# The joint of a ternary feed-forward stage and a windowed attention stage: closing order, values, a sum of squares and a table load moved

## The chip, the cores and the metric

The kernel runs on one core of a Trainium2 chip. The metric is the device time of one execution in microseconds (us). Five engines share the work: TensorE (PE, matmuls), VectorE (DVE), ScalarE (ACT), GpSimd (POOL) and SyncE (SP, which only issues DMAs here).

## What is computed

The input X is 4096 rows of 256 (two sequences of 2048). Four residual parts follow one another: a retention network of two layers with its feed-forward parts, a ternary feed-forward part, a windowed attention, and the same ternary feed-forward part again. Cut to what the change touches:

```python
def _ternary_linear(x, w):
    ...
    rms = jnp.sqrt(jnp.sum(x * x, axis=-1, keepdims=True)) / jnp.sqrt(jnp.asarray(d, x.dtype))
    x_norm = x / (rms + EPS)
    return jnp.einsum('bsd,fd->bsf', x_norm, w_q)
h = jax.nn.gelu(_ternary_linear(x, w_up), approximate=False)
return _ternary_linear(h, w_down)
...
q = _rms_norm(q)
k = _rms_norm(k)
q = _apply_rotary(q, cos, sin)
k = _apply_rotary(k, cos, sin)
...
att = jax.nn.softmax(scores, axis=-1)
y = jnp.einsum('bhqk,bhkd->bhqd', att, v_full)
...
x = x + _L0_ffn_ref(_layernorm(x, axis=-1), L0_ffn_w_up, L0_ffn_w_down)
x = x + _L0_attn_b_ref(_layernorm(x, axis=-1), ...)
x = x + _L0_ffn_ref(_layernorm(x, axis=-1), L0_ffn_w_up, L0_ffn_w_down)
```

The attention has 16 query heads and 4 key heads of 16 columns and looks back 64 rows.

## The kernel before

X stays in on-chip memory. Every stage is a block of one program for each engine, and the stages follow one another: a stage begins when every engine has finished the one before (the joint). Inside a stage the order on each engine is written out by hand, and semaphores couple the engines. POOL collects the engines at a joint and lets them go.

**The ternary stage** (`ffn`, called with `window` for the first of the two) walks over NB = 8 blocks of 512 rows. A step g works on block b = g - 2 on the hidden side and normalises block g - 1; each step has MF = 8 parts m, one for 128 of the 1024 hidden columns. For a part, PE makes the hidden product (L857), ACT applies Gelu twice (L758, L759), DVE subtracts (L548), and PE adds the part to the output (L870, `down_product`) two parts later. Beside that ACT and POOL square the hidden values; PE adds the squares over the rows with ones (L905, `square_sums`, in two halves), ACT copies the result (L787), PE transposes it (L919, `transpose_sums`), DVE copies it (L560), POOL takes its root (L448, L452), and DVE takes the reciprocal (L566) and adds the scaled output into X (L577, four instructions of 256 columns).

**At its end** this stage already does work of the attention, which takes tiles of 128 rows; tiles 0 and 1 are begun here. For each of them PE projects queries, keys and values (L929, `first_project`), and ACT takes the squares (L793) and a raw copy (L796, `first_raw`). For tile 0 DVE sums the squares (L641), POOL takes the power -0.5 of 20 columns (L356) and multiplies by a gain (L359, `first_head_scales`), DVE rotates (L650, L653, L662) and writes the scaled heads (L666, `first_pad`). POOL copies the values of both tiles in three instructions each (L366, L369, L372, `first_values`).

In step 10 (`NB + 2`), the last but one, the written order on PE is: part 6 of the last block's output product, second half of the square sums, part 7 of the output product, transpose of the sums, projection of tile 1. DVE's order is: output of block 6 (L577), rotation (at m = 3), copy of the sums (L560, m = 5), `first_pad` (m = 6), then in step 11 reciprocal and output of block 7. The function `closing(g)` is true only in the last stage, and gives there another order by `last_down`.

**The attention stage** (`window_attention`, NT = 32 tiles) runs step n with tiles in different phases: `project` (L2589) of tile n - 2, keys and queries transposed by PE (L2608, L2619) and copied by ACT (L2460, L2454) for tile n - 3, keys moved by POOL (`even_keys`, L2230, L2231) for tile n - 3, `head_scales` by POOL (L2218, L2222) for n - 2, `pad` on DVE (L2351) for n - 3, scores (L2641), exponentials and the rest after that. `made(n, k)` says that tiles below k have had this done in the stage before. Step 3 is the first that has work: PE transposes tile 0 and projects tile 2, POOL moves the keys of tile 0 and then takes the head scales of tile 1, DVE sums the squares of tile 1 (L2333), copies tile 2's projection (L2340) and rotates tile 1 (L2322, L2325, L2344). In step 4 DVE pads tile 1, and PE transposes it. ACT's block begins with an exponential of one column (L2552) that brings in the function table of the exponential, since the ternary stage used Gelu's.

## Time and profile before

| | us |
|---|---|
| median of three runs | 1459.81 |
| lowest and highest of them | 1459.66, 1461.78 |
| time of the profiled execution | 1459.51 |
| its span, first to last instruction | 1457.6 |
| PE busy | 1405.6 |
| DVE, ACT, POOL busy | 1059.7, 927.1, 809.0 |
| mean granted clock of PE | 0.994 |

The span is what the trace shows; 1.9 us of the execution lie around it. An engine's busy time can be near the span and still say little about a joint, where all engines wait for the last of them. In the timelines a row is one instruction, or several alike; the brackets at its end hold the idle time before it and what ended it. An engine's name with a q is its sequencer, seen through a semaphore that it raised.

### The profile page before, as it was taken

Reading aid. Unit: us, or ns where it says so; the run is one execution under the profiler, and the core shown is the slowest. Engines: PE = TensorE matmul, PEld = TensorE weight load, DVE = VectorE, ACT = ScalarE, POOL = GpSimd, SP = SyncE. Lnnn points to the kernel's source line nnn. Section 1 sums busy time; section 2 is a strip of 40 time slices with the busy share of each in tenths; the row PEclk is TensorE's granted clock in tenths of the full one; section 3 lists DMA queues with packets and bytes.
Section 4 is the critical chain, followed back from the end, with each engine's and each line's share of the span. In section 5 each row is a group of like instructions: output and inputs, shape, how many; then the busy total and the mean of one; then the engine's idle time right before and its main releaser. Section 6 shows DMA issues by size and latency. Waiting matters only on the chain. (4 is left out here: it accounts for less than half of the span.)

```text
span 1457.6 us, 36349 instructions
## 1 busy us (share of the span) xinstructions
PE 1405.6 (96%) x13004; PEld 1169.9 (80%) x13004; DVE 1059.7 (73%) x2347; ACT 927.1 (64%) x1872; POOL 809.0 (55%) x884
## 2 busy tenths in 40 slices
PE   6999999999998999999999999998899999989998
PEld 5777877889896788888889888887677777768886
DVE  6877777565546887776664669775899999966775
ACT  4665565565552655555655558776778887767775
POOL 3766666322113657665552437776666666636774
PEclk9999999999999999999999999999999999999999
DMA  7000000100001000000311010000000000000101
GB/s 228 31 2 1 0 1 2 37 1 1 1 1 58 2 2 1 0 2 2 103 43 29 1 41 1 1 0 1 2 2 0 0 0 0 0 2 10 36 29 44
DMA packets 21176, 26.28 MB, mean 18 GB/s; under 512 B 1984, under 2 KB 19136, under 8 KB 20928
## 3 DMA queue, kind: packets, MB, share of 16 engines
q1 hardware_dynamic: 20768, 24.61, 5.2%
q8 instruction: 75, 1.23, 0.3%
q14 instruction: 45, 0.37, 0.1%
q10 hardware_dynamic: 288, 0.07, 0.0%
HBM read 20.48 MB, written 4.19 MB: 17 GB/s over the span
## 5 line engine op out<-in xcount | busy, mean ns | idle before, releaser
L548 DVE TENSOR_TENSOR ffn_h_lo<-ffn_h,ffn_h_hi 128x512 fp32r<-128x512 f32 x112 | 86.2, 770 | 122.2 <-ACT ffn_h_hi L759 122.2
L758 ACT ACTIVATE ffn_h<-ffn_hp,c_b 128x512 f32<-128x512 f32 x112 | 77.3, 690 | 145.2 <-PE ffn_hp L857 144.7
L548 DVE TENSOR_TENSOR ternary_ffn_h_lo<-ternary_ffn_h,ternary_ffn_h_hi 128x512 fp32r<-128x512 f32 x128 | 110.8, 865 | 76.4 <-ACT ternary_ffn_h_hi L759 76.3
L2218 POOL TENSOR_TENSOR win_rms<-win_sq_sum,win_minus_half 128x20 f32<-128x20 f32 x31 | 109.8, 3540 | 65.0 <-DVE win_sq_sum L2333 65.0
L1253 POOL TENSOR_TENSOR ret_qk<-ret_qk,ret_qk_sin 128x512 f32<-128x512 f32 x64 | 82.7, 1292 | 99.4 <-DVE ret_qk_sin L1360 98.7
L870 PE MATMUL ternary_ffn_yp<-down_ternary,ternary_ffn_h_hi 128*128 128x256 f32 x512 | 132.4, 291 | 0.0
L870 PE MATMUL ternary_ffn_yp<-down_ternary,ternary_ffn_h_lo 128*128 128x256 f32 x512 | 127.7, 282 | 0.0
L870 PE MATMUL ffn_yp<-down_hi,ffn_h_hi 128*128 128x256 f32 x448 | 127.5, 285 | 0.0
L1259 POOL TENSOR_TENSOR ret_rstd<-ret_sums,ret_minus_half 128x16 f32<-128x16 f32 x32 | 103.7, 3240 | 42.7 <-DVE ret_sums L1402 42.7
L870 PE MATMUL ffn_yp<-down_hi,ffn_h_lo 128*128 128x256 f32 x448 | 125.0, 279 | 0.0
L870 PE MATMUL ffn_yp<-down_lo,ffn_h_hi 128*128 128x256 f32 x448 | 125.0, 279 | 0.0
L444 POOL TENSOR_TENSOR ternary_ffn_h_sq<-ternary_ffn_h_sq 128x512 f32<-128x512 f32 x61 | 94.3, 1554 | 42.6 <-ACT ternary_ffn_h_sq L765 38.5
L758 ACT ACTIVATE ternary_ffn_h<-ternary_ffn_hp 128x512 f32<-128x512 f32 x128 | 76.5, 598 | 54.5 <-PE ternary_ffn_hp L857 48.4
L857 PE MATMUL ternary_ffn_hp<-xt_hi,up_ternary 128*128 128x512 f32 x256 | 102.3, 400 | 5.3 <-DVEq L735 5.0
L870 PEld LDWEIGHTS ternary_ffn_yp<-down_ternary,ternary_ffn_h_hi 128*128 128x128 f32 x512 | 97.1, 190 | 7.3 <-issue 3.8
L857 PE MATMUL ternary_ffn_hp<-xt_lo,up_ternary 128*128 128x512 f32 x256 | 102.4, 400 | 0.0
L870 PEld LDWEIGHTS ternary_ffn_yp<-down_ternary,ternary_ffn_h_lo 128*128 128x128 f32 x512 | 97.4, 190 | 3.2
L1357 DVE TENSOR_TENSOR ret_qk<-ret_pj,rotary 128x512 f32<-128x512 f32 x64 | 44.2, 691 | 72.7 <-PE ret_pj L1751 72.7
L2363 DVE TENSOR_REDUCE wa_minus_top<-wa_sc 128x4 fp32r<-128x512 f32 x128 | 82.2, 684 | 16.2 <-PE wa_sc L2641 16.2
L857 PE MATMUL ffn_hp<-xt_hi,up_hi 128*128 128x512 f32 x224 | 89.0, 397 | 2.4 <-DVEq L735 2.4
L1370 DVE TENSOR_TENSOR ret_probs<-ret_sc,causal 128x1024 f32<-128x1024 f32 x64 | 78.4, 1224 | 15.8 <-issue 10.8
L857 PE MATMUL ffn_hp<-xt_lo,up_hi 128*128 128x512 f32 x224 | 88.8, 397 | 0.0
(331 smaller groups left out, 4683.0 us busy)
## 6 DMA issues: line engine op xcount, KB each, us to landing
staging<-in_w SPq DMA_DIRECT2D x4, 1024.0 KB, 6.1
ffn_x_in<-in_x SPq DMA_DIRECT2D x8, 512.0 KB, 3.7
X<-in_x SPq DMA_DIRECT2D x7, 512.0 KB, 8.0
out<-X SPq DMA_DIRECT2D x7, 512.0 KB, 2.9
staging<-in_wqkv SPq DMA_DIRECT2D x2, 768.0 KB, 4.5
rotary<-in_rotary SPq DMA_DIRECT2D x1, 1024.0 KB, 6.8
staging<-in_w_up SPq DMA_DIRECT2D x1, 1024.0 KB, 5.1
staging<-in_w_down SPq DMA_DIRECT2D x1, 1024.0 KB, 7.6
```

The costliest lines, as they stand in the source:

```text
L444: nc.gpsimd.tensor_tensor(h_sq[:, m, :], h_sq[:, m, :], h_sq[:, m + 1, :], ALU.add).then_inc(sq_added, 1)
L548: nc.vector.tensor_tensor(h_lo[:, m % R, :], h[:, m % R, :], h_hi[:, m % R, :].bitcast(F32), ALU.subtract).then_inc(h_ready, 1)
L758: nc.scalar.activation(h[:, m % R, :], hp[m % 2][:, :], fn, bias=bias)
L857: last = nc.tensor.matmul(hp[m % 2][:, :], w[:, j, m * P:(m + 1) * P], x[:, k, j, :], start=(n == 0), stop=(n == len(todo) - 1))
L870: last = nc.tensor.matmul(yp[k][t // 2][:, (t % 2) * D:(t % 2 + 1) * D], x[:, m % R, t * P:(t + 1) * P], w[:, m, :], start=(m == 0 and t % ...
L1253: nc.gpsimd.tensor_tensor(qk[:, r, :, :, :], qk[:, r, :, :, :], qk_sin[:, r, :, :, :], ALU.add).then_inc(qk_done, 1)
L1259: nc.gpsimd.tensor_tensor(rstd[:, :], sums[:, 1, :], minus_half[:, :], ALU.pow).then_inc(rstd_done, 1)
L1357: nc.vector.tensor_tensor(qk[:, r, :, :, :], src, cos, ALU.mult)
L1370: nc.vector.tensor_tensor(pr[:, at % 2, :, :, :], sc[:, :, 0:HT].rearrange("p h (j n) -> p h j n", j=NG), causal[:, :].unsqueeze(1).unsque ...
L2218: nc.gpsimd.tensor_tensor(rms[:, 1, :], sq_sum[:, :], minus_half[:, :], ALU.pow).then_inc(rms_work, 1)
L2363: nc.vector.tensor_reduce(minus_top[:, g, :], sc[:, g, :].rearrange("p (c m) -> p c m", m=P), axis=AX.X, op=ALU.max, negate=True).then_inc ...
```

## The change

- `closing(g)` is true in the stage before the attention too. So PE's order in step 10 becomes: half of part 6 of the output product, second half of the square sums, the other half of part 6, transpose of the sums, projection of tile 1, part 7.
- POOL copies the values of tile 0 ahead of its head scales in step 9, and no longer copies those of tile 1 in this stage; the attention stage does that in its step 5.
- The squares of tile 1 are summed by DVE at the end of the ternary stage (`second_square_sums`, after `first_pad`), no longer in step 3 of the attention.
- ACT loads the exponential's table after the raw copy of tile 1 in step 10, no longer at the head of the attention's block.
- The keys of tile 0 are moved by ACT (`first_even_keys`, two copies) instead of by POOL.

```diff
--- before.py
+++ after.py
@@ -243,7 +243,7 @@
 
         def closing(g):
 
-            return out_dram is not None and isinstance(g, int) and g == NB + 2
+            return (out_dram is not None or window is not None) and isinstance(g, int) and g == NB + 2
 
         def step_of(g):
 
@@ -498,10 +498,8 @@
                         if not adds_late(b):
                             add_squares(b, 4)
                     if window is not None and final_block(b):
+                        first_values(0)
                         first_head_scales()
-                    if window is not None and final_block(b - 1):
-                        for n in range(2):
-                            first_values(n)
                     if window is not None and at_third(g):
                         window_gain()
 
@@ -641,6 +639,12 @@
                 nc.vector.tensor_reduce(window["sq_sum"][:, :], window["sq"][:, :, :],
                                         axis=AX.X, op=ALU.add).then_inc(sq_sum_done, 1)
 
+            def second_square_sums():
+
+                dve.wait_ge(sq_done, 2)
+                dve.wait_ge(head_work, 1)
+                nc.vector.tensor_reduce(window["sq_sum"][:, :], window["sq"][:, :, :], axis=AX.X, op=ALU.add)
+
             def first_rotate():
 
                 dve.wait_ge(raw_done, 1)
@@ -675,6 +679,7 @@
                     first_rotate()
                 if g == NB + 2 and window is not None and m == 6:
                     first_pad()
+                    second_square_sums()
                 if g == 2 and m == 4 and values is not None:
                     centre_values()
                 if g == 3 and m < len(halves):
@@ -801,6 +806,7 @@
                     first_raw(0)
                 if g == NB + 2 and window is not None and m == 5:
                     first_raw(1)
+                    nc.scalar.activation(table_set[:, :], ident[:, 0:1], ACT.Exp)
                 if g == 3 and m == 0 and halves:
                     act.wait_ge(prefetched, 16 * len(loads))
                     if values is not None:
@@ -911,6 +917,8 @@
                 if m == 0:
                     down_product(NB - 1, MF - 2, 1, between=lambda: square_sums(NB - 1, 1))
                     transpose_sums(NB - 1)
+                    if window is not None:
+                        first_project(1)
                 if m == 1:
                     down_product(NB - 1, MF - 1, 1)
 
@@ -967,8 +975,6 @@
                             transposes(g - 1, 1)
                         if ternary and m == 5 and live(b - 1, NB):
                             transpose_sums(b - 1)
-                        if window is not None and final_block(b - 1) and m == 5:
-                            first_project(1)
                         if ternary and m == 7 and live(b, NB):
                             square_sums(b, 0)
                         if m >= 2 and to_do(b):
@@ -2043,7 +2049,6 @@
         next_stats = sb("next_stats", [P, 2 * TB, 6])
         next_work = sb("next_work", [P, 3, 2 * TB])
         powers = sb("powers", [P, 2, 2 * TB])
-        table_set = sb("table_set", [P, 1])
         qt = sb("qt", [P, 2, PAIRS, NC, P])
 
 
@@ -2161,8 +2166,8 @@
             pool.sem_inc(scale_done, TB)
             pool.sem_inc(rms_work, 1)
             pool.sem_inc(rms_done, 1)
-            pool.sem_inc(v_work, 4)
-            pool.sem_inc(v_done, 2)
+            pool.sem_inc(v_work, 2)
+            pool.sem_inc(v_done, 1)
 
             def next_scales():
 
@@ -2235,9 +2240,9 @@
                     n = U * i + k
                     if final_tile(n - 3):
                         even_keys(n - 3, k - 3)
-                    if live(n - 4, NT) and not made(n - 4, 2):
+                    if live(n - 4, NT) and not made(n - 4, 1):
                         values(n - 4, k - 4)
-                    if live(n - 3, NT) and not final_tile(n - 3):
+                    if live(n - 3, NT) and not final_tile(n - 3) and not at_start(n - 3):
                         even_keys(n - 3, k - 3)
                     if live(n - 2, NT) and not made(n - 2, 1):
                         head_scales(n - 2)
@@ -2253,7 +2258,8 @@
             dve.sem_inc(padded_done, 1)
             dve.sem_inc(xt_ready, TB)
             dve.sem_inc(raw_done, 2)
-            for ready in (sq_sum_done, rot_done, rot_sum_done):
+            dve.sem_inc(sq_sum_done, 2)
+            for ready in (rot_done, rot_sum_done):
                 dve.sem_inc(ready, 1)
             for ready in (stats_done, mv_done, xn_done):
                 dve.sem_inc(ready, TB)
@@ -2413,7 +2419,7 @@
                         output_low(n - 6)
                     if live(n - 4, NT):
                         row_max(n - 4, 2)
-                    if live(n - 2, NT) and not made(n - 2, 1):
+                    if live(n - 2, NT) and not made(n - 2, 2):
                         square_sums(n - 2)
                     if live(n - 2, NT) and not made(n - 2, 3):
                         raw_out(n - 2, k - 2)
@@ -2466,6 +2472,12 @@
                 nc.scalar.activation(sq[:, :, 0:WD], pj[:, 0:NH * WD].rearrange("p (h d) -> p h d", d=WD), ACT.Square,
                                      scale=WD ** -0.5).then_inc(sq_done, 1)
 
+            def first_even_keys():
+
+                act.wait_ge(kt_done, 1)
+                nc.scalar.activation(kt[:, 0, 2, :], kt[:, 0, 0, :], ACT.Copy)
+                nc.scalar.activation(kt[:, 2 % R, 3, :], kt[:, 0, 1, :], ACT.Copy).then_inc(kt_moved, 1)
+
             def probs_out(n, g):
                 act.wait_ge(pt_full, WKV * n + (TOPS.index(g) if final_tile(n) else g) + 1)
                 at_least(act, y_full, n)
@@ -2521,6 +2533,8 @@
                     if live(n - 3, NT):
                         keys_out(n - 3, k - 3)
                         queries_out(n - 3, k - 3)
+                    if at_start(n - 3):
+                        first_even_keys()
                     if live(n - 5, NT) and not final_tile(n - 5):
                         probs_out(n - 5, 3)
                     if live(n - 6, NT):
@@ -2549,7 +2563,6 @@
 
             act.sem_inc(xt_hi_done, TB)
             act.sem_inc(sq_done, 2)
-            nc.scalar.activation(table_set[:, :], ident[:, 0:1], ACT.Exp)
             skewed(act, body, N, first=2, last=2)
 
         @block.tensor
```

## Rows read from the trace of the kernel before

**Rows 1.** The page: the whole execution
```profile
span 1457.6 us, 36349 instructions
```

**Rows 2.** Windows: stretch, its us, busy us of each engine, PEclk (granted clock), DMA
```profile
1017.30:1020.50 3.20, 3.16 (x13) 2.76 (x14) 0.51 (x1) 2.03 (x4) 1.48 (x3) 0.51 0.02 5
...
1048.20:1056.90 8.70, 8.70 (x100) 6.81 (x96) 8.13 (x20) 7.00 (x20) 5.83 (x10) 1.00 0.01 2
```

**Rows 3.** Timeline of PE at the joint: start, us, line, operation, [idle before]
```profile
1009.42 0.28 PE L870 MATMUL ternary_ffn_yp<-down_ternary,ternary_ffn_h_lo 128*128 128x256 f32 x1
...
1009.90 0.28 PE L870 MATMUL ternary_ffn_yp<-down_ternary,ternary_ffn_h_lo 128*128 128x256 f32 x1
...
1010.11 1.08 PE L905 MATMUL ternary_ffn_sqp<-ternary_ffn_h_sq,ternary_ffn_ones 128*32 128x128 f32 x32
...
1012.19 0.27 PE L919 MATMUL ternary_ffn_sqp<-c_ident,ternary_ffn_sq_sums 128*128 128x128 f32 x1
...
1013.18 0.34 PE L929 MATMUL ternary_ffn_tp<-win_qkv_hi,xt_lo 128*128 128x384 f32 x1
...
1017.34 0.45 PE L2608 MATMUL wa_tr<-c_ident,win_padded 128*128 128x128 f32 x1 [3.81 <-DVEq L2254]
...
1020.04 0.52 PE L2589 MATMUL wa_pj<-win_qkv_hi,xt_lo 128*128 128x384 f32 x1
...
1023.92 0.34 PE L2608 MATMUL wa_tr<-c_ident,win_padded 128*128 128x128 f32 x1 [1.73 <-DVE win_padded L2351]
```

**Rows 4.** Timeline of POOL at the joint
```profile
1008.03 3.56 POOL L356 TENSOR_TENSOR win_rms<-win_sq_sum,win_minus_half 128x20 f32<-128x20 f32 x1 [1.20 <-DVE win_sq_sum L641]
...
1012.74 1.19 POOL L448 TENSOR_TENSOR ternary_ffn_rms<-ternary_ffn_mean_square,ternary_ffn_powers 128x4 f32<-128x4 f32 x1 [0.65 <-DVE ternary_ffn_mean_square L560]
...
1016.34 0.24 POOL L372 COPY win_v_even<-win_raw 64x64 f32<-64x64 f32 x1 [0.17 <-POOL win_v_even L369]
...
1017.06 0.15 POOL L2158 MEMSET wa_powers<- 128x8 f32 x2 [0.48 <-SPq L2028]
...
1019.40 3.56 POOL L2218 TENSOR_TENSOR win_rms<-win_sq_sum,win_minus_half 128x20 f32<-128x20 f32 x1
```

**Rows 5.** Timeline of DVE at the joint
```profile
1011.45 0.56 DVE L653 TENSOR_TENSOR win_rot<-win_raw,staging 128x160 f32<-128x160 f32 x2
...
1012.50 0.16 DVE L560 COPY ternary_ffn_mean_square<-ternary_ffn_sqp 128x4 f32<-128x4 f32 x1 [0.49 <-PE ternary_ffn_sqp L919]
...
1014.41 0.18 DVE L566 RECIPROCAL ternary_ffn_inv_rms<-ternary_ffn_rms 128x4 f32<-128x4 f32 x1 [0.73 <-POOL ternary_ffn_rms L452]
...
1014.62 1.66 DVE L577 SCALAR_TENSOR_TENSOR X<-ternary_ffn_yp,ternary_ffn_inv_rms,X 128x256 f32<-128x256 f32 x4
...
1018.19 0.51 DVE L2333 TENSOR_REDUCE win_sq_sum<-win_sq 128x20 f32<-128x340 f32 x1 [1.91 <-POOLq L2162]
...
1023.37 0.49 DVE L2351 TENSOR_TENSOR win_padded<-win_rot,win_rms 128x320 f32<-128x320 f32 x1 [0.36 <-POOL win_rms L2222]
```

**Rows 6.** Timeline of ACT at the joint
```profile
1013.89 0.48 ACT L796 ACTIVATE win_raw<-ternary_ffn_tp 128x384 f32<-128x384 f32 x1
...
1017.20 1.28 ACT L2552 ACT_TABLE_LOAD   x1 [2.82 <-PEq L125]
...
1018.49 0.20 ACT L2552 ACTIVATE wa_table<-c_ident 128x1 f32<-128x1 f32 x1
...
1020.59 0.44 ACT L2466 ACTIVATE win_sq<-wa_pj 128x320 f32<-128x320 f32 x1 [1.25 <-PE wa_pj L2589]
```

**Rows 7.** Windows: start of the last stage
```profile
1307.80:1314.00 6.20, 6.20 (x17) 4.99 (x18) 2.98 (x8) 5.48 (x10) 0.68 (x4) 0.50 0.00 0
```

**Rows 8.** Timeline of PE: first matmul of each ternary stage
```profile
868.39 0.50 PE L857 MATMUL ternary_ffn_hp<-xt_hi,up_ternary 128*128 128x512 f32 x1 [2.38 <-DVEq L735]
...
1307.79 0.79 PE L857 MATMUL ternary_ffn_hp<-xt_hi,up_ternary 128*128 128x512 f32 x1 [2.60 <-DVEq L735]
```

**Rows 9.** Timeline of POOL, sixth step of the attention stage
```profile
1034.81 3.54 POOL L2218 TENSOR_TENSOR win_rms<-win_sq_sum,win_minus_half 128x20 f32<-128x20 f32 x1 [2.33 <-DVE win_sq_sum L2333]
```

## The prediction

> **What bounds the kernel now.** The page gives the span, 1457.6 us [rows 1]. The windows view says what a gain at the joint is worth: one attention tile takes 8.7 us, and PE is busy in all of them at full clock [rows 2]. From some tile on the attention is PE's own work, so what is won before that stays won, one for one, and what is won on another engine inside it is worth nothing. The place to read is therefore the joint and the first tiles after it, in the timelines of the four engines.
>
> There the reader sees two chains. *First, the end of the ternary stage.* PE is done at 1013.52 (last row at 1013.18, 0.34 long) and starts the next stage at 1017.34, after 3.81 idle [rows 3]. Two engines are late. DVE copies the sums at 1012.50, as soon as PE has transposed them (1012.19) [rows 3, 5]; POOL takes the root from 1012.74 [rows 4]; DVE's reciprocal follows at 1014.41 and the four output instructions end at 14.62 + 1.66 = 1016.28 [rows 5]. POOL then copies values until 1016.34 + 0.24 = 1016.58, and its first instruction of the attention is at 1017.06, 0.48 later [rows 4]. So POOL's copies are the last, and DVE's output is 0.30 behind them.
> *Second, the second tile.* PE waits 1.73 us for its padded heads and transposes them at 1023.92 [rows 3]. DVE padded at 1023.37, having waited 0.36 for POOL's head scales [rows 5], which POOL began at 1019.40 and which took 3.56 [rows 4]. Had POOL been early, DVE could have padded at 1023.37 - 0.36 = 1023.01, since it had itself been held by ACT's squares of tile 2 (1020.59), and these by the end of PE's projection (last matmul at 1020.04, 0.52 long) [rows 3, 6]. PE does that at a granted clock of 0.51, that is mostly at 1.2 GHz instead of 2.4 [rows 2].
>
> **The end of the stage, part by part.** *Closing order.* The square sums start at 1010.11 after all eight matmuls of part 6 [rows 3]. Four of them go behind the sums; four take about 0.5 (starts at 1009.42 and 1009.90 [rows 3]), so the sums start near 1009.6 and end near 1010.6, and the four matmuls end near 1011.1. ACT's copy of the sums lay somewhere in the 1.0 between their end, 1011.19, and the transpose, 1012.19, so at the very worst the transpose comes at 1011.6; I take 1011.2. Either way DVE is still rotating until 1011.45 + 0.56 = 1012.01 [rows 5], so its copy moves from 1012.50 to about 1012.0: 0.5 won, not 1.0. POOL is free for the root when tile 0's head scales and gain are through, 1012.74 - 0.65 = 1012.09 [rows 4]. So the root moves from 1012.74 to 1012.2, the reciprocal from 1014.41 to 1013.9, and DVE's last output ends at 1015.75. Part 7 of the product now comes last on PE, yet ends by about 1013.5 as PE's total is unchanged; the output's first half needs it only at 1014.1.
> *Values of tile 0* (three copies of 0.24 and two waits of 0.17 between, 1.05) go ahead of the head scales. POOL was idle for 1.20 there, ahead of 1008.03, waiting for DVE [rows 4]: 0 to 0.1 late. *Values of tile 1* leave the stage. Together POOL's tail of six copies, 2.3 us, is gone and POOL is done before DVE. They come back in step 5 of the attention: 1.05 more on POOL before it moves tile 2's keys. There POOL is idle 2.33 ahead of the head scales at 1034.81 [rows 9]; DVE's raw copy of tile 3 waits for them too, and the same idle stretch covers it. Nothing; without cover, 1.05.
> *Second sum of squares*, 0.51 by its row [rows 5]. Behind it on DVE are the reciprocal and the output, hence the whole joint. It waits for ACT's squares of tile 1. The projection stands 1.0 earlier, so its last matmul ends near 1012.6 instead of 1013.52, and ACT's squares (0.44 by those of tile 2 [rows 6]) near 1013.1. DVE has its copy, an addition and the padding (0.16 and two of 0.49 [rows 5]) done by about 1013.2, the sum by 1013.7, and DVE would have waited for POOL until 1013.9 anyway: nothing, with 0.2 in hand.
> *Table load*, 1.28 and 0.20 [rows 6]: from about 1013.5, when the raw copy ends (it ended at 1014.37), to 1015.0. DVE holds the joint until 1015.75, so it is hidden with 0.8 in hand.
> *The joint.* DVE is last, at 1015.75 instead of POOL at 1016.58. From POOL's last copy to its first instruction 0.48 passed, including POOL's own closing; behind DVE I bound this by 0.3 and 0.48. So the attention starts at 1016.05 to 1016.25 instead of 1017.06. I take 1.0 won; 0.8 is the other end.
> The Trainium skill ("ScalarE: Activation LUTs", section "What ACT_TABLE_LOAD costs") says that a switch of tables costs about 2.66 us, of which 1.28 is the load and the rest a drain. The rows show 1.28 and the next activation 0.01 after it [rows 6], but ACT had been idle before, so they can't deny a drain behind running work. By the page ACT would be done near 1016.4, and 0.6 of the 1.0 would be lost; the rival below takes the same delay as a mechanism.
>
> **After the joint, counted from the stage's start.** *POOL.* Its head scales of tile 1 now wait for neither the sum nor the keys. They start once POOL has set its counters, somewhere between 0.3 and 2.34 after its first instruction (now 1019.40 - 1017.06 = 2.34); I take 0.6, as it has only short instructions to issue. Padding follows the start of the scales by 1023.37 - 1019.40 = 3.97 [rows 4, 5], so POOL would allow it at 4.6 after its first instruction instead of 6.31: 1.7 earlier.
> *ACT.* Without the load the first key copy is 0.8 earlier; the two copies of keys taken from POOL cost it 0.2 each by the smallest activation's row (0.20 [rows 6]). PE needs them only after projection and masks: hidden.
> *PE and DVE.* Nothing in the change shortens the projection of tile 2, so this chain keeps its length and gives only the 0.36 that DVE waited, unless the clock is another. At half clock PE took 1020.56 - 1017.34 = 3.22 [rows 3]; at full clock at most half of it, 1.6, would be won, and a single projection matmul shrinks only from 0.52 to 0.34 (the last of tile 2 and of tile 1 [rows 3]). I take 1.2 more, and POOL's 1.7 is just enough to let it through: 1.6 in all.
> *The clock.* It was at half after 3.81 idle [rows 2, 3] and after 2.60, and full after 2.38, where the first matmul took 0.50 against 0.79 [rows 7, 8]. The changed kernel idles PE for 1013.5 to 1016.3, some 2.9. So either may come, or a fall shortly after the restart. Ends: 0.4 and 1.6; I take the middle, 1.0.
>
> **The sum.** 1.0 + 1.0 = 2.0 (1.2 to 2.6). On the profiled execution: span 1455.6, time 1457.5. Its time was 0.3 below the median, so for the median 1459.81 - 2.0 = **1457.8**. A measurement of this kernel can tell about 0.2%, 2.9 us, from no change, so this counts as within.
>
> **Rivals.**
> *The clock changes at the next joint too.* PE ran at 0.50 from 1307.8 to 1314.0 there [rows 7]. If, with everything shifted by 2 us, that spell is as short as this joint's 3.2, half of the 3.0 between is won: 2.0 + 1.5, 1456.3. For it: the same idle time gave different spells. Against: nothing in the change shortens the idle time of 2.60 there.
> *A new wait takes the old one's place.* ACT's squares come 0.4 or more later than I place them, DVE sits on the second sum, and the reciprocal behind it is no earlier; at the same time the clock falls as now. Won: 0.3 at the joint, 0.4 after it: 1459.1.
> *ACT holds the joint*: the table load behind running work takes longer than the 0.8 in hand. The rows bound it only by one load's own 1.28 again, which leaves 1.28 - 0.8 = 0.5 lost: 1458.3. For it: no row shows a load right behind work. Against: none shows more than 1.28 either.
> *A clock spell the other way*: one more of 3.2 us at the start of a ternary stage, as at 1307.79 but not at 868.39 [rows 8]: 1.4 won, 1.6 lost, 1460.0.
> *The table doesn't stay (slower).* The attention's block now opens with plain copies. If the table is loaded anew wherever its exponentials begin, it costs 1.28 before the first, and 1.28 in each of the six passes of the loop, all on the way from scores to PE's transposes: 1459.8 - 2.0 + 7 x 1.28 = 1466.8. It decides from the third reload on. Against: the trace has one load at this joint and none in the loop now.
>
> **Chances.** Forecast 0.48; next joint's clock as well 0.22; new wait 0.13; ACT last 0.05; clock the other way 0.09; table reloaded 0.03. The range takes the forecast's ends, the shorter spell and the new wait: 1455.7 to 1459.6; what is left out is the two slower cases and the tails. Faster by over 0.2% means below 1456.9: the 0.22, and 0.06 of the forecast's best end, 0.28. Slower by over 0.2%: 0.03. Within: 0.69.
>
> **What would show it.** The joint: DVE's last output near 1015.75, POOL's first instruction near 1016.1. Order: transpose of sums near 1011.2, DVE's copy directly behind the rotation, its second sum without a wait of over 0.1. One table load, between the raw copy and the joint. Tile 1: head scales 0.6 after POOL's first instruction; padding at 1021.0 to 1022.2; its row tells by the releaser (POOL, or none) which chain was last. The granted clock from the restart to the end of the projection tells 0.4 from 1.6. I am wrong if a steady tile is no longer 8.7 us or if POOL's values hold it in step 5.

## The result, and the profile after

| | before | changed |
|---|---|---|
| median of 13 runs | 1459.86 | 1457.45 |
| lowest and highest | 1458.67, 1461.78 | 1455.69, 1458.96 |
| span of the profiled execution | 1457.6 | 1455.3 |

The ratio of the two is 0.9982, with a 95% interval of 0.9975 to 0.9989: the change makes the kernel faster by 2.4 us, which the interval tells from nothing, and by less than the 0.2% that the prediction took as the bound of a change. In a second comparison, beside the experiments, the ratio was 0.9982 again (0.9973 to 0.9991); the medians of that one are 1459.76 and 1456.82, 2.94 apart.

The line numbers of the changed kernel differ by a few. TensorE at the joint, before (the one row of it not shown yet, which serves as zero in what follows) and then changed; columns are start, length, engine, line, operation, idle before:

```profile
1007.43 0.64 PE L905 MATMUL ternary_ffn_sqp<-ternary_ffn_h_sq,ternary_ffn_ones 128*32 128x128 f32 x16
```

```profile
1008.88 0.64 PE L911 MATMUL ternary_ffn_sqp<-ternary_ffn_h_sq,ternary_ffn_ones 128*32 128x128 f32 x16
...
1011.09 1.08 PE L911 MATMUL ternary_ffn_sqp<-ternary_ffn_h_sq,ternary_ffn_ones 128*32 128x128 f32 x32
...
1012.68 0.27 PE L927 MATMUL ternary_ffn_sqp<-c_ident,ternary_ffn_sq_sums 128*128 128x128 f32 x1
...
1017.77 0.30 PE L2621 MATMUL wa_tr<-c_ident,win_padded 128*128 128x128 f32 x1 [2.81 <-DVEq L2259]
...
1019.46 0.33 PE L2602 MATMUL wa_pj<-win_qkv_hi,xt_lo 128*128 128x384 f32 x1
...
1022.99 0.33 PE L2621 MATMUL wa_tr<-c_ident,win_padded 128*128 128x128 f32 x1 [1.56 <-DVE win_padded L2357]
```

The zero is the first matmul of the first half of the last block's square sums. It lies 1.45 later in the changed kernel's trace, for a reason of its own (below), so times at the joint are compared from it. The second half of the sums starts 2.21 behind it instead of 2.68 (1010.11 [rows 3]); the transpose of the sums at 3.80 instead of 4.76; PE then idles 2.81 instead of 3.81, and transposes tile 1 at 14.11 instead of 16.49.

GpSimd and VectorE of the changed kernel:

```profile
1009.61 3.56 POOL L356 TENSOR_TENSOR win_rms<-win_sq_sum,win_minus_half 128x20 f32<-128x20 f32 x1
...
1013.61 1.24 POOL L448 TENSOR_TENSOR ternary_ffn_rms<-ternary_ffn_mean_square,ternary_ffn_powers 128x4 f32<-128x4 f32 x1
...
1017.49 0.15 POOL L2163 MEMSET wa_powers<- 128x8 f32 x2 [2.19 <-SPq L2034]
...
1018.21 3.56 POOL L2223 TENSOR_TENSOR win_rms<-win_sq_sum,win_minus_half 128x20 f32<-128x20 f32 x1 [0.58 <-DVEq L2261]
...
1021.85 0.49 POOL L2227 TENSOR_TENSOR win_rms<-win_rms,staging 128x20 f32<-128x20 f32 x1
...
1033.87 3.54 POOL L2223 TENSOR_TENSOR win_rms<-win_sq_sum,win_minus_half 128x20 f32<-128x20 f32 x1 [1.24 <-DVE win_sq_sum L2339]
```

```profile
1013.37 0.15 DVE L558 COPY ternary_ffn_mean_square<-ternary_ffn_sqp 128x4 f32<-128x4 f32 x1
...
1014.52 0.51 DVE L646 TENSOR_REDUCE win_sq_sum<-win_sq 128x20 f32<-128x340 f32 x1
...
1015.33 0.18 DVE L564 RECIPROCAL ternary_ffn_inv_rms<-ternary_ffn_rms 128x4 f32<-128x4 f32 x1 [0.30 <-POOL ternary_ffn_rms L452]
...
1015.54 1.66 DVE L575 SCALAR_TENSOR_TENSOR X<-ternary_ffn_yp,ternary_ffn_inv_rms,X 128x256 f32<-128x256 f32 x4
...
1022.44 0.49 DVE L2357 TENSOR_TENSOR win_padded<-win_rot,win_rms 128x320 f32<-128x320 f32 x1 [0.19 <-POOL win_rms L2227]
```

The copy of the sums (1013.37) now stands directly behind the rotation, with no idle time; before it waited 0.49 [rows 5]. The root starts at 4.73 from zero instead of 5.31, the second sum (1014.52) stands without a wait between padding and reciprocal, and VectorE ends at 15.54 + 1.66 = 1017.20, 8.32 from zero instead of 8.85. GpSimd has nothing left behind its root, and its first instruction of the attention is at 8.61 instead of 9.63 (1017.06 [rows 4]). Its head scales start 0.72 behind that, not 2.34, and the padding of tile 1 comes 4.95 behind it, not 6.31.

ScalarE with the table load, and the granted clock (PEclk, the third number from the end) in three stretches:

```profile
1014.38 0.49 ACT L801 ACTIVATE win_raw<-ternary_ffn_tp 128x384 f32<-128x384 f32 x1
...
1014.89 1.28 ACT L809 ACT_TABLE_LOAD   x1
...
1016.18 0.20 ACT L809 ACTIVATE ternary_ffn_table<-c_ident 128x1 f32<-128x1 f32 x1
```

```profile
869.50:872.90 3.40, 3.40 (x9) 2.59 (x9) 0.68 (x2) 2.93 (x6) 3.19 (x7) 0.50 0.72 225
...
1017.70:1019.80 2.10, 2.03 (x13) 1.62 (x15) 0.00 (x0) 1.16 (x4) 1.59 (x1) 1.00 0.03 8
...
1306.80:1309.80 3.00, 3.00 (x7) 2.33 (x8) 0.00 (x0) 2.35 (x4) 0.00 (x0) 0.50 0.00 0
```

**Where the 2.33 of the two spans is.** TensorE's first matmul of the first ternary stage:

```profile
869.21 0.57 PE L863 MATMUL ternary_ffn_hp<-xt_hi,up_ternary 128*128 128x512 f32 x1 [2.38 <-DVEq L740]
```

- *Up to the zero, +1.45.* 0.82 of it is there at this matmul already (869.21 against 868.39 [rows 8]), so it stems from the stages before, which the change doesn't touch. The other 0.63 follows behind it, where the clock was at half from 869.5 to 872.9 and was full before. From this matmul to the zero it is 139.66 to 139.68 us in the six of all 14 traces with such a spell, and 139.00 to 139.04 in the eight without.
- *From the zero to tile 5, -2.41* (transposed at 1055.89 here, 1056.85 before).
- *From tile 5 to the last stage's first matmul, -0.18* (1306.65 against 1307.79, 1.14 in all). This is the change's too. The stretch takes 250.92 to 250.94 in the four traces in which the table is loaded at the head of the attention, and 250.74 to 250.78 in the ten others; the move of the load, undone alone, brings the longer value back. It is spread over the steady tiles (26.02 for three of them against 26.00). Why is open.
- *The last stage, -1.19.* Its half-clock spell was 3.4 us here and 6.8 before [rows 7]. From its first matmul to the end of its last it is 142.1 in the six traces with 3.4 us, 142.9 to 143.3 in the six with 6.8, and 141.4 in the two with none.

Sum: +1.45 - 2.41 - 0.18 - 1.19 = -2.33. So the two profiled executions differ by more than the change, in both directions; its own work is 2.41 + 0.18 = 2.59, and that the whole differs by nearly as much is because the two other terms almost cancel.

### The profile page after: what moved, and what is told of

Same layout as the page of the kernel before. It is cut to its first block and busy times, and to the rows that moved or that the text cites. A ratio compares the mean times of both kernels' runs of the same rounds, so it can differ in the third digit from the quotient of the medians.

```text
span 1455.3 us, 36348 instructions
## 1 busy us (share of the span) xinstructions
PE 1403.6 (96%) x13004; PEld 1167.9 (80%) x13004; DVE 1058.4 (73%) x2347; ACT 926.3 (64%) x1874; POOL 807.6 (55%) x882
```

## The experiments

The theory was: 1.0 at the joint by the closing order and the values together, the rest by GpSimd's earlier head scales of tile 1, which the second sum, the keys and the table load all held. The first rival was that the gain is the clock's: a shorter idle time keeps TensorE at 2.4 GHz. To keep it from blurring the single steps, most kernels have ten matmuls more behind PE's last work of the stage; nobody reads their result:

```diff
+            def keep_busy(pieces):
+
+                pe.wait_ge(h_read, MF * NB)
+                for _ in range(pieces):
+                    nc.tensor.matmul(hp[0][:, :], up[0][:, 0, 0:P], xt_hi[:, 0, 0, :], start=True, stop=True)
...
             skewed(pe, body, N, first=3 if begun else 2, last=2)
+            if window is not None:
+                keep_busy(10)
```

### Fillers at the joint, at all joints, and in the kernel before

> The changed kernel, with ten matmuls of 512 columns more on TensorE behind its last work of the ternary stage (their result is used by nobody). Theory: the trace of the changed kernel has the joint at full clock after 2.81 us idle, and the gain there is 2.4 (1.0 at the joint, 1.4 after it). The fillers cut the idle time to about 0.6, so the clock holds in every run; the padding of tile 1 stays 4.95 us after GpSimd's first instruction, and the median is at most 0.4 below the changed kernel's 1457.45, by the runs in which the clock had fallen. Rival (the clock carries the gain only by chance, and falls in most unprofiled runs): median 1.0 or more below. Rival (fillers hold the joint): later joint, slower.

> The changed kernel again, beside the three with fillers on the same chip: 1457.5, 2.4 below the kernel before.

Measured: fillers 1456.88 (11 runs; ratio to the kernel before 0.9987, 0.9978 to 0.9996), changed kernel 1456.82 (11 runs), before 1459.76 (30 runs). PE's idle time fell to 0.54 and the padding came 4.97 behind GpSimd's first instruction, as expected, but nothing was gained:

```profile
1015.98 0.30 PE L2629 MATMUL wa_tr<-c_ident,win_padded 128*128 128x128 f32 x1 [0.54 <-DVEq L2267]
```

The changed kernel's own trace of this run tells what the clock costs there, since it fell shortly after PE's restart (PEclk is the third number from the end):

```profile
1017.60:1021.00 3.40, 3.40 (x26) 2.13 (x28) 1.26 (x4) 1.03 (x4) 3.32 (x2) 0.50 0.00 0
```

```profile
1018.71 0.52 PE L2602 MATMUL wa_pj<-win_qkv_hi,xt_lo 128*128 128x384 f32 x1
...
1016.25 0.15 POOL L2163 MEMSET wa_powers<- 128x8 f32 x2 [2.19 <-POOLq L125]
...
1021.23 0.49 DVE L2350 TENSOR_TENSOR win_rot<-win_rot 128x320 f32<-128x320 f32 x1
...
1021.76 0.49 DVE L2357 TENSOR_TENSOR win_padded<-win_rot,win_rms 128x320 f32<-128x320 f32 x1
```

The projection's last matmul starts 2.46 behind GpSimd's first instruction instead of 1.97, and is 0.52 long instead of 0.33. VectorE is what holds the padding now (addition until 1021.72, padding at 1021.76, no wait for GpSimd), 5.51 behind GpSimd's first instruction instead of 4.95. So a clock that falls 1.05 behind PE's restart costs the changed kernel 0.56 here, and not the 1.2 between the prediction's two ends; no trace of it shows the clock at half from the restart on, as in the kernel before.

For all joints there were three fillers more in each dense feed-forward stage and these in the attention:

```diff
             skewed(pe, body, N, first=2, last=2)
+            for _ in range(6):
+                nc.tensor.matmul(sc[:, 3, 0:D], ident_r[:, :], out_w[0][:, 0, :], start=True, stop=True)
```

> As the kernel with fillers at this joint, with three fillers more at the end of each of the two dense feed-forward stages and six of 256 columns at the end of the attention, so that TensorE idles 1.7 to 1.9 us there instead of 2.4 to 2.8. Theory: each spell at half clock of 3.41 us costs about 1.4 us where TensorE is the bound; the changed kernel's trace has three of them (at 442.8, 869.5 and 1306.4), so without any the time is near 1453.5 and the trace shows full clock from the first stage to the last. Rival: the clock falls after idle times of 1.8 too: no spell goes, 1457.

Measured: 1455.35 (8 runs, 1454.19 to 1457.17; ratio to before 0.9976, 0.9966 to 0.9987). Of the changed kernel's three spells (442.8, 869.5, 1306.4) two are gone, and one stayed (at 443.5 here, behind 1.76 us of idle time), so the full clock "from the first stage to the last" was missed:

```profile
443.60:446.80 3.20, 3.20 (x12) 2.72 (x11) 2.37 (x7) 0.00 (x0) 0.94 (x1) 0.50 0.81 327
...
868.00:872.00 4.00, 3.65 (x19) 2.79 (x18) 1.85 (x5) 3.93 (x8) 3.33 (x7) 1.00 0.74 225
...
1304.00:1312.00 8.00, 7.09 (x39) 5.89 (x40) 4.92 (x11) 7.37 (x14) 1.62 (x6) 1.00 0.00 1
```

By its median this is the fastest kernel of the study, 1.5 below the changed one, where 4 was expected; the two intervals overlap. The price of 1.4 a spell was too high: by the stretches above a spell of 3.4 us costs 0.6 at the head of the first ternary stage and 0.75 in the last stage.

> The kernel before with the same fillers at all joints. It tells the change's worth apart from the clock. Theory: at full clock the kernel before pads tile 1 no earlier, since its GpSimd chain (3.97 us behind 1019.40) holds it, so the change is still worth 1.0 at the joint and 1.36 after it: this kernel is 2.3 us slower than the changed one with the same fillers. Rival (the change pays by the clock alone): less than 1.2 us between the two.

Measured: 1458.96 (11 runs; ratio to before 0.9999, 0.9990 to 1.0008), so 3.6 slower than the changed kernel with the same fillers. With the fillers the clock held through the projection (its last matmul 0.33 long), and yet the kernel before pads tile 1 no earlier:

```profile
1016.58 0.15 POOL L2168 MEMSET wa_powers<- 128x8 f32 x2 [0.48 <-SPq L2038]
...
1018.92 3.56 POOL L2228 TENSOR_TENSOR win_rms<-win_sq_sum,win_minus_half 128x20 f32<-128x20 f32 x1
...
1022.89 0.49 DVE L2361 TENSOR_TENSOR win_padded<-win_rot,win_rms 128x320 f32<-128x320 f32 x1 [1.39 <-POOL win_rms L2232]
```

The padding is 6.31 behind GpSimd's first instruction as in [rows 4, 5], only that VectorE now waits 1.39 for GpSimd instead of 0.36. The rival falls: the clock alone gives the kernel before nothing at this place, and the change gives 15.92 - 13.63 = 2.29 with the clock at full in both. By tile 5 the difference is 3.55: this trace has a half-clock spell of 6.8 us from 1024.2, which that of the changed kernel with fillers has not. Whether the change has a part in that spell is open. It may have one: PE idles 2.75 ahead of tile 1's transpose here and in the kernel with sum, keys and load undone (below), and both have a spell of 6.8 there, while it idles 1.42 in the changed kernel with either set of fillers, and neither has one.

### One part undone at a time

All with the fillers at the joint, unless the table says otherwise. Root, first instruction (GpSimd's first of the attention) and tile 5 (its transpose) are from the zero; head scales and padding of tile 1 are from GpSimd's first instruction. The last column is a half-clock spell at the joint or in the first tiles, with its start from the zero.

| kernel | zero | root | first instruction | head scales | padding | tile 5 | spell |
|---|---|---|---|---|---|---|---|
| before (no fillers) | 1007.43 | 5.31 | 9.63 | 2.34 | 6.31 | 49.42 | 3.4 at 9.6 |
| before, fillers at all joints | 1006.97 | 5.31 | 9.61 | 2.34 | 6.31 | 50.63 | 6.8 at 17.2 |
| changed (no fillers) | 1008.88 | 4.73 | 8.61 | 0.72 | 4.95 | 47.01 | none |
| changed (no fillers), second trace | 1007.64 | 4.73 | 8.61 | 0.72 | 5.51 | 47.57 | 3.4 at 9.9 |
| changed, fillers | 1007.04 | 4.72 | 8.66 | 0.72 | 4.97 | 47.06 | none |
| changed, fillers at all joints | 1006.71 | 4.72 | 8.66 | 0.72 | 4.97 | 47.08 | none |
| order undone | 1008.16 | 5.31 | 9.17 | 0.72 | 4.97 | 47.57 | none |
| values of tile 0 undone | 1007.19 | 4.72 | 8.66 | 0.72 | 4.94 | 48.00 | 3.4 at 17.9 |
| values of tile 1 undone | 1007.66 | 4.72 | 8.66 | 0.72 | 4.94 | 48.06 | 3.4 at 18.2 |
| both values undone | 1006.90 | 4.72 | 9.08 | 0.72 | 4.95 | 49.26 | 6.8 at 16.7 |
| second sum undone | 1007.56 | 4.72 | 8.66 | 1.73 | 5.70 | 50.36 | 10.2 at 14.5 |
| keys undone | 1007.67 | 4.72 | 8.66 | 1.43 | 5.40 | 49.30 | 6.8 at 16.7 |
| table load undone | 1007.66 | 4.72 | 8.66 | 0.72 | 4.97 | 48.11 | 3.4 at 18.2 |
| sum, keys and load undone | 1006.77 | 4.72 | 8.66 | 2.34 | 6.31 | 50.21 | 6.8 at 17.5 |

Each kernel with a part undone was run once, so only its trace counts. The times are 1456.96 (order), 1457.38, 1458.00 and 1457.31 (values of tile 0, of tile 1, both), 1459.12 (sum), 1458.12 (keys), 1458.22 (load) and 1458.30 (all three), beside 1459.03 to 1460.67 for the kernel before; single times can't order steps of 0.4 to 0.7.

**Order.** `closing(g)` as before, and the projection of tile 1 back at m = 5:

```diff
-            return (out_dram is not None or window is not None) and isinstance(g, int) and g == NB + 2
+            return out_dram is not None and isinstance(g, int) and g == NB + 2
```

> The changed kernel with fillers at the joint, and PE's closing order as before. All times are from the first matmul of the first half of the last block's square sums. With the order changed: the root at 4.72, the reciprocal at 6.44, GpSimd's first instruction of the attention at 8.66, the padding of tile 1 4.97 later. Theory (the order is worth 0.5 by the root): root at 5.3, reciprocal at 7.0, first instruction at 9.2, padding 4.97 after it. Theory's second part (the second sum now stands in front of the reciprocal and waits for the later projection): 0.1 more, 9.3. Rival (GpSimd or ScalarE would hold the joint anyway): below 8.8.

```profile
1013.47 1.19 POOL L448 TENSOR_TENSOR ternary_ffn_rms<-ternary_ffn_mean_square,ternary_ffn_powers 128x4 f32<-128x4 f32 x1 [0.65 <-DVE ternary_ffn_mean_square L558]
...
1017.33 0.15 POOL L2171 MEMSET wa_powers<- 128x8 f32 x2 [2.23 <-POOLq L125]
...
1014.75 0.51 DVE L646 TENSOR_REDUCE win_sq_sum<-win_sq 128x20 f32<-128x340 f32 x1 [0.34 <-ACT win_sq L798]
```

The order is worth 0.51, all through the root (1013.47, waiting 0.65 for VectorE as before). The second sum now waits 0.34 for ScalarE's squares, as the second part of the theory had it, but delays the joint by hardly anything (VectorE ends at 8.88 from the zero instead of 8.85 before).

**Values.** For tile 0, behind the root again:

```diff
-                        first_values(0)
                         first_head_scales()
+                    if window is not None and final_block(b - 1):
+                        first_values(0)
```

> The changed kernel with fillers at the joint, with the values of tile 0 copied behind the root again (those of tile 1 stay in the attention). Times from the first matmul of the first half of the square sums. Theory: GpSimd's root is done at 6.4 and three copies take 1.05 more, to 7.4, while VectorE's output lasts until 8.32: the joint stays at 8.66. The head scales of tile 0 start 0.1 earlier. Rival (every copy taken off GpSimd's end counts): joint 1.0 later.

> The changed kernel with fillers at the joint, with the values of tile 1 copied by GpSimd at the end of the ternary stage again (those of tile 0 stay ahead). Theory: as with tile 0's alone, the joint stays at 8.66, and the fifth tile's keys come where they did, since the attention's step 5 covers them either way. Rival (step 5 doesn't cover them): later tiles 0.5 to 1.0 earlier than with the changed kernel.

> The changed kernel with fillers at the joint, with all six copies of values behind the root again. Theory: GpSimd ends at 6.4 + 2.3 = 8.7 instead of VectorE at 8.32, and with its own closing of 0.48 the attention starts at 9.15: 0.5 late. So either half of the move is free, and only the two together pay. Rival: 8.66 still, because another engine holds the joint.

```profile
1014.34 0.23 POOL L372 COPY win_v_even<-win_raw 64x64 f32<-64x64 f32 x1 [0.17 <-POOL win_v_even L369]
...
1015.85 0.15 POOL L2172 MEMSET wa_powers<- 128x8 f32 x2 [1.27 <-SPq L2043]
...
1013.85 1.66 DVE L576 SCALAR_TENSOR_TENSOR X<-ternary_ffn_yp,ternary_ffn_inv_rms,X 128x256 f32<-128x256 f32 x4
```

```profile
1015.27 0.23 POOL L372 COPY win_v_even<-win_raw 64x64 f32<-64x64 f32 x1 [0.17 <-POOL win_v_even L369]
...
1015.98 0.15 POOL L2173 MEMSET wa_powers<- 128x8 f32 x2 [0.48 <-SPq L2044]
...
1013.55 1.66 DVE L577 SCALAR_TENSOR_TENSOR X<-ternary_ffn_yp,ternary_ffn_inv_rms,X 128x256 f32<-128x256 f32 x4
```

With tile 0's copies alone GpSimd ends at 1014.57, 0.94 before VectorE (1015.51), and its next instruction is 0.34 behind VectorE's end. With all six it ends at 1015.50, 0.29 behind VectorE, and its own 0.48 follow. So either half of the move changes nothing by itself; together they are worth 0.42. With the order's 0.51 that is 0.93, of the 0.95 between the kernels before and changed with the fillers. That step 5 of the attention covers tile 1's values is shown by the changed kernel itself: GpSimd's idle time ahead of 1033.87 is 1.24 instead of 2.33 [rows 9], and tile 5 kept the full -2.41. The kernels with the values of tile 0 and of tile 1 undone agree: both have a spell of 3.4 us at the same place, and tile 5 comes no earlier where step 5 has no values to copy (48.06 from the zero, against 48.00 where it has).

**Second sum, keys, table load.**

```diff
                     first_pad()
-                    second_square_sums()
...
-                    if at_start(n - 3):
-                        first_even_keys()
...
+            nc.scalar.activation(table_set[:, :], ident[:, 0:1], ACT.Exp)
             skewed(act, body, N, first=2, last=2)
```

> The changed kernel with fillers at the joint, with the squares of tile 1 summed in the attention again. Theory: nothing at the joint (8.66), since VectorE waited for the root anyway; after it VectorE sums from 1.1 to 1.6 after GpSimd's first instruction, the head scales start at 1.7 instead of 0.72, and the padding comes at 6.0 instead of 4.97. Rival (the sum in front of the reciprocal costs the joint what it saves later): the joint at 8.4 or less.

> The changed kernel with fillers at the joint, with the keys of tile 0 moved by GpSimd again. Theory: GpSimd waits for ScalarE's key copy (ends 0.9 after GpSimd's first instruction) and moves them in 0.45, so the head scales start at 1.5 instead of 0.72 and the padding comes at 5.75 instead of 4.97; the joint stays at 8.66. Rival (ScalarE's two copies delay its squares of tile 2 by as much): 4.97 or less.

> The changed kernel with fillers at the joint, with the table load at the head of the attention again. Theory: the joint stays at 8.66; ScalarE is free for its first copy at 1.6 after GpSimd's first instruction, has done keys, queries and the two moved copies at 2.7 and starts the squares of tile 2 there instead of at 2.50; the padding is late by 0.1 to 0.3 (5.1 to 5.3). Rival (the load at the joint's end delays the joint, by the page's 2.66 us): joint at 8.4 or less here. Second rival: a load moved ahead is worth its whole 1.28: padding at 6.2.

> The changed kernel with fillers at the joint, with table load, keys of tile 0 and second sum all as before: what is left is the closing order and the values. Theory: the joint at 8.66; the head scales of tile 1 start at 2.34 after GpSimd's first instruction as before, and the padding comes at 6.31, at either clock. So these three are worth 1.34 together, though they would sum to 1.9 to 2.1 singly. Rival (the projection's clock sets the padding): 5.0 to 5.3 with the fillers.

With the sum, the keys, the load, and all three undone, in this order:

```profile
1016.22 0.15 POOL L2170 MEMSET wa_powers<- 128x8 f32 x2 [2.25 <-POOLq L125]
...
1017.95 3.56 POOL L2230 TENSOR_TENSOR win_rms<-win_sq_sum,win_minus_half 128x20 f32<-128x20 f32 x1 [1.58 <-DVE win_sq_sum L2345]
...
1021.92 0.49 DVE L2363 TENSOR_TENSOR win_padded<-win_rot,win_rms 128x320 f32<-128x320 f32 x1 [0.95 <-POOL win_rms L2234]
```

```profile
1016.33 0.15 POOL L2171 MEMSET wa_powers<- 128x8 f32 x2 [2.24 <-POOLq L125]
...
1017.76 3.56 POOL L2231 TENSOR_TENSOR win_rms<-win_sq_sum,win_minus_half 128x20 f32<-128x20 f32 x1
...
1021.73 0.49 DVE L2365 TENSOR_TENSOR win_padded<-win_rot,win_rms 128x320 f32<-128x320 f32 x1 [0.51 <-POOL win_rms L2235]
```

```profile
1016.32 0.15 POOL L2171 MEMSET wa_powers<- 128x8 f32 x2 [2.25 <-POOLq L125]
...
1021.29 0.49 DVE L2365 TENSOR_TENSOR win_padded<-win_rot,win_rms 128x320 f32<-128x320 f32 x1
```

```profile
1015.43 0.15 POOL L2170 MEMSET wa_powers<- 128x8 f32 x2 [2.25 <-POOLq L125]
...
1017.77 3.55 POOL L2230 TENSOR_TENSOR win_rms<-win_sq_sum,win_minus_half 128x20 f32<-128x20 f32 x1
...
1021.74 0.49 DVE L2363 TENSOR_TENSOR win_padded<-win_rot,win_rms 128x320 f32<-128x320 f32 x1 [1.39 <-POOL win_rms L2234]
```

The joint is at 8.66 in all four: neither the sum in front of the reciprocal nor the load in ScalarE's tail costs it anything. The head scales start where expected (1.73, 1.43, 2.34). The padding follows 3.97 behind them in each of these, 5.70, 5.40 and 6.31: I had expected 6.0 and 5.75, having added the whole delay to 4.97, where 0.72 + 3.97 = 4.69 lies 0.28 below it. That 0.28 is slack: in the changed kernel the projection's chain on VectorE ends at the same time. The load alone is worth 0.00 at the padding, less than the 0.1 to 0.3 expected. This value holds to 0.03: in this trace PE's last matmul of the projection starts 1.96 behind GpSimd's first instruction and in that of the changed kernel with fillers 2.12, and where the values are undone it is 1.96 with the padding at 4.94. The load's two rivals (a drain that delays the joint, and the whole 1.28 won behind it) both fall. What it is worth besides is the 0.18 over the steady tiles.

The three are worth 0.73, 0.43 and 0.00 singly and 1.34 together. So the parts don't simply add up: with sum, keys and load all undone, ScalarE's load holds the key copy, the key copy holds GpSimd's keys, and these hold the scales, up to the 2.34 of before.

## Why the prediction was right

**The end of the stage** came as worked out, step by step (predicted, then measured, from the zero): transpose of the sums 3.8 and 3.80, copy of the sums 4.6 and 4.49, root 4.8 and 4.73, reciprocal 6.5 and 6.45, VectorE's end 8.32 and 8.32, GpSimd's first instruction 8.6 to 8.8 and 8.61. The cover of each free part held: values of tile 0 in GpSimd's idle 1.20 (its scales began 0.13 later, one copy having taken 0.47 instead of 0.23), sum in VectorE's wait (0.30 of it is left at 1015.33), load behind 0.82 of VectorE's output (ScalarE ends at 1016.38).

**The table's drain.** The load begins at 1014.89, 0.02 behind the raw copy's end (1014.38 + 0.49), takes 1.28, and the next activation starts 0.01 later. So here no drain of 1.4 follows or precedes a load behind running work. The trace gives one load's own time, where the Trainium skill ("ScalarE: Activation LUTs", section "What ACT_TABLE_LOAD costs") gives about 2.66 us for a switch.

**After the joint** the term came out between its ends, and larger than the 1.0 taken, the middle of 0.4 and 1.6: measured were 1.36 at full clock and 0.80 in the trace where it fell. At full clock I had GpSimd allow 1.7. Its scales start at 0.72, not 0.6, since its own counters are set early but it waits 0.58 for one that VectorE sets (row 1018.21), and the gain's multiplication took 0.49 (1021.85), not 0.23, so it allowed 1.36. VectorE's chain alone, ready 0.19 before its padding, would have given 1.55, as worked out. At half clock I had the whole projection slow, as before; that case, the 0.4, was not met, since in the trace where the clock fell it did so after the restart.

**Put at nothing** was the load's move within the attention; it brought 0.18. The change's worth by the traces is so 1.02 + 1.36 + 0.18 = 2.56 (2.59 taken at tile 5), or 1.02 + 0.80 + 0.18 = 2.00 where the clock falls, against my 1.2 to 2.6 with 2.0 as the forecast. The two differences of medians are 2.41 and 2.94. Each has a 95% interval 2 us wide or more, so they don't tell 2.0 from 2.6, and how often the clock falls in executions without a profile is not known.

**Luck** is in the profiled execution's 1457.14 and span of 1455.3, against 1457.5 and 1455.6 predicted: two clock terms that the sum had left out, of opposite sign, nearly cancelled there.

**The sign of the clock's part** was reasoned the right way (a gain at this place only if GpSimd is out of the way first), and the kernel before with fillers shows it: full clock there, and no gain.

**The rivals.** Shorter spell at the next joint: it came in the profiled execution (3.4 instead of 6.8, 1.19), and so did its counterpart, the spell more at the head of a ternary stage (869.5), which with what was late before it made +1.45. In the changed kernel's second trace the last stage's spell was 6.8 and the first ternary stage had none, so both are a matter of the single execution. New wait: not there. ScalarE last: not there. Table reloaded: one load at the joint, none in the loop. A steady tile takes 8.67 us, as before.

## What to carry to other kernels

At a joint of stages, list when each engine is done and remove work from the last one only until the next is last: here two moves of values were free singly and 0.42 together, because VectorE ended only 0.3 before GpSimd. Work taken out of a chain is worth what the next chain leaves: after the joint 1.62 was taken from the head scales and 1.36 arrived. And where single executions differ by spells of another clock, compare traces from a common event close to the change: up to the joint the steps of the same code repeated to 0.01 us from trace to trace, and the paddings at full clock to 0.03, while medians needed a dozen runs to show 2.4.

## What was not expected of the hardware

**TensorE's clock also fell in the first steps of the attention**, where PE works with breaks. It idles 0.61 to 2.75 us ahead of tile 1's transpose. Of 14 traces eight, all with fillers, show a spell at 1.2 GHz that begins between 1022 and 1026; the kernels without fillers have none in three traces, but two of these had their spell at the joint instead. With the second sum undone it lasted 10.2 us:

```profile
1022.20:1032.20 10.00, 8.54 (x55) 5.64 (x55) 5.93 (x14) 5.10 (x14) 5.76 (x9) 0.50 0.00 1
...
1022.47 0.48 PE L2627 MATMUL wa_tr<-c_ident,win_padded 128*128 128x128 f32 x1 [2.31 <-DVE win_padded L2363]
...
1032.32 0.34 PE L2627 MATMUL wa_tr<-c_ident,win_padded 128*128 128x128 f32 x1
```

From tile 1's transpose to tile 2's it is 9.85 there, against 7.31 in the changed kernel without fillers (1022.99 to 1030.30). With spells of 3.4 and 6.8 it was 8.33 (load undone) and 9.10 (keys undone). Such spells could explain why the fillers at the joint brought nothing in the median: they keep the clock at the restart, where it is worth 0.56, and a spell a few us later costs 1.0 to 2.5. That is not shown, since the one trace of that kernel has none there.

Whether the spell came went with the idle time ahead of tile 1's transpose: in all four traces with 1.87 or more (keys, sum, all three undone, and the kernel before with fillers), in four of the six with 1.55 to 1.73, and in none of the four with 1.42 or less. So what a change does to that idle time may be worth more than its own few tenths. No run isolates this.

**The table load took no more than its 1.28 us**, also right behind a running copy (1014.89 above).
